# A graph layer on one core: sums in five pieces under a gate, and the products of h moved into the last groups

## The reference

```python
h = jnp.maximum(_layernorm(x, axis=-1), 0.0)                        # 6250 nodes x 64
msg_in = concatenate([h[src], h[dst], edge_attr_32], axis=-1)       # 206250 edges x 160
messages = swish(msg_in @ W1 + b1) @ W2 + b2
att = softmax(swish(msg_in @ Wa1 + ba1) @ Wa2 + ba2, axis=0)        # over all edges
aggregated = segment_sum(messages * att, dst, 6250)
out = x + swish(concatenate([h, aggregated]) @ Wu1 + bu1) @ Wu2 + bu2
```

## Time and profile before

| | |
|---|---|
| runs | 2853.89, 2855.56, 2858.01 us; median 2855.56 |
| profiled execution | 2869.82 us, of which the span is 2868.1 |
| busy | PE 50%, POOL 54%, DVE 36%, ACT 32% of the span |
| granted TensorE clock | 0.629 on average; 0.9 in the first twentieth, then 0.5 to 0.6 |
| moved by DMA | 227.10 MB, 79 GB/s |

### The profile page before, as it was taken

One profiled execution on the slowest core, in us unless ns is written; L12 is line 12 of the kernel. 1 busy time (PEld: TensorE's weight loads), 2 busy tenths in 40 slices (PEclk: granted clock), 3 DMA queues, 4 the chain that ended last, 5 costly groups with the idle time before them and its releaser, 6 DMA issues.

```text
span 2868.1 us, 26391 instructions
## 1 busy us (share of the span) xinstructions
PE 1438.3 (50%) x7070; PEld 1210.3 (42%) x7070; DVE 1031.7 (36%) x2240; ACT 923.1 (32%) x1132; POOL 1540.5 (54%) x1628
## 2 busy tenths in 40 slices
PE   4334454554545455544445554554545444554459
PEld 3334444443444344444344444444444343444444
DVE  6133333343333333333333433333443333333353
ACT  3233333333333333333333333333333333333322
POOL 4355555555555555555555555555555555555520
PEclk9966656566655656565655556556566656566665
DMA  4333333333333333333333333322333333323301
GB/s 123 98 78 83 87 79 78 77 79 78 88 83 79 78 79 77 78 91 80 78 78 80 77 82 89 78 78 77 80 78 87 84 78 78 79 77 78 87 25 23
DMA packets 112463, 227.10 MB, mean 79 GB/s; under 512 B 55880, under 2 KB 76156, under 8 KB 102204
## 3 DMA queue, kind: packets, MB, share of 16 engines
q1 hardware_dynamic: 60376, 121.03, 16.2%
q0 software_dynamic: 51584, 105.75, 15.3%
q10 hardware_dynamic: 484, 0.10, 0.0%
HBM read 218.75 MB, written 8.00 MB: 79 GB/s over the span
## 4 chain that ended last, share of the span: by engine, by line
another core or an unknown queue 57%; DVE 23%; issue 11%; PE 4%; DVEq 3%; DMA 1%; ACT 0%; SPq 0%; ACTq 0%
DVE prod L841 5%; DVE bank L857 5%; DVE v L848 4%; DVE hot L823 3%; DVE lg L843 2%; DVEq L829 1%; PE bank L699 1%; PE bank L713 1%; PE bank L704 1%; PE bank L623 1%; DVE gmax L862 1%; DVE lgb L900 1%; DVE zp L834 1%; PE bank L571 0%
## 5 line engine op out<-in xcount | busy, mean ns | idle before, releaser
L395 POOL DMA_INDIRECT p_rows<-p_tab,src_i x1612 | 1522.3, 944 | 1218.0 <-DMA src_i<-src 716.5
L612 PE MATMUL bank<-q_win,comb 128*128 128x128 f32 x3224 | 862.7, 397 | 939.5 <-issue 925.4
L612 PEld LDWEIGHTS bank<-q_win,comb 128*128 128x128 f32 x3224 | 705.5, 293 | 1066.4 <-issue 1063.8
L501 ACT ACTIVATE s<-bank 128x512 f32<-128x512 f32 x403 | 237.2, 589 | 1736.1 <-DVE bank L857 1735.2
L832 DVE SCALAR_TENSOR_TENSOR acc<-acc,fade,bank 65x96 f32 x81 | 25.1, 310 | 1663.4 <-remote 1613.3
L623 PE MATMUL bank<-hot,v 128*65 128x96 f32 x3224 | 410.6, 306 | 235.0 <-issue 204.4
L623 PEld LDWEIGHTS bank<-hot,v 128*65 128x65 f32 x3224 | 394.2, 185 | 257.7 <-issue 244.4
L857 DVE TENSOR_TENSOR bank<-bank,p_rows 128x512 f32<-128x512 f32 x403 | 278.2, 690 | 12.4 <-PE bank L612 6.5
L471 ACT ACTIVATE comb<-dst_b,row_of 96x1024 f32<-96x1024 int32 (+1 forms) x162 | 217.8, 1344 | 11.4 <-DMA dst_b<-dst_row 11.4
L477 ACT ACTIVATE comb<-comb,ones 96x1024 f32<-96x1024 f32 (+1 forms) x162 | 218.8, 1351 | 2.7
L823 DVE TENSOR_TENSOR hot<-bank,rel 128x960 f32<-128x960 f32 x162 | 185.2, 1144 | 0.0
(11 more groups left out here) (104 smaller groups left out, 449.7 us busy)
## 6 DMA issues: line engine op xcount, KB each, us to landing
dst_b<-dst_row SPq DMA_DIRECT2D x80, 960.0 KB
p_rows<-p_tab,src_i POOLq DMA_INDIRECT x1612
comb<-efT SPq DMA_DIRECT2D x80, 320.0 KB, 3.5
q_win<-q_tab SPq DMA_DIRECT2D x81, 48.0 KB, 2.5
p_tab<-th SPq DMA_DIRECT2D x12, 256.0 KB, 2.3
q_tab<-hot SPq DMA_DIRECT2D x12, 256.0 KB
x_sb<-x SPq DMA_DIRECT2D x3, 512.0 KB, 5.6
out<-s SPq DMA_DIRECT2D x12, 128.0 KB, 2.0
```

Of the source, the lines that this page charges most:

```text
L395: pool.indirect_dma_start(p_rows[:, a, t * H2:(t + 1) * H2], None, p_tab, bass.IndirectOffsetOnAxis(src_i[:, a, t:t + 1], 0)).then_inc(gat ...
L501: nc.scalar.activation(silu_rows(a, q), halves(ps_z[q][:]), ACT.Silu).then_inc(silu_ok, 1)
L612: last = nc.tensor.matmul(ps_z[q][:, (t % TQ) * H2:(t % TQ + 1) * H2], comb[:, a, t * P:(t + 1) * P], q_win[:, a, :], start=True, stop=True)
```

## The change

*Sums in pieces.* The 20 products of `sums` become five calls of four, one per quarter, which add up in the same bank; `hot` and `v` are made per quarter too. Each piece (except in the last group) first waits for a gate: three of the four rows of a quarter of a later group must have landed. For this the fourth row of each quarter gets a semaphore of its own, `gath_end`. Pieces 1 to 4 of g-2 and piece 0 of g-1 are spread over PE's group; `add_part` is now that of g-2 and stands behind logits 3. ACT's `weights` move from behind silu 2 to behind silu 3.

*Products of h.* `own_part` leaves the tail. Its 6272 columns are multiplied in 25 pieces of 256 columns in groups 75 to 79, one per quarter, into the quarter's own bank after its silu; ACT copies each back over `hT`, and the next products in that bank wait for the copy. In the tail DVE adds the products of `acc` to them (`whole_u`), and tanh and silu read `hT`.

*Loops.* Groups 74 to 80 are written out, where 78 to 80 were.

```diff
+        gath_end = [[sem(f"gath_end{a}{q}") for q in range(NQ)] for a in range(2)]
...
+        def own_unit(g, q):
+            u = (g - (LAST - 5)) * NQ + q if isinstance(g, int) and not is_last(g) else -1
+            return [(u, u * 2 * P, min(NP, (u + 1) * 2 * P))] if u >= 0 else []
...
-                    sp.wait_ge(gath[a][NQ - 1], per(a, g, 16 * TQ))
+                    sp.wait_ge(gath[a][NQ - 1], per(a, g, 16 * GQ))
+                    sp.wait_ge(gath_end[a][NQ - 1], per(a, g, 16))
...
-IndirectOffsetOnAxis(src_i[:, a, t:t + 1], 0)).then_inc(gath[a][q], 16)
+IndirectOffsetOnAxis(src_i[:, a, t:t + 1], 0)).then_inc(gath[a][q] if t % TQ < GQ else gath_end[a][q], 16)
...
+            def own_copy(g, q):
+                for u, c0, c1 in own_unit(g, q):
+                    act.wait_ge(uh_done, u + 1)
+                    nc.scalar.activation(hT[0:U, c0:c1], ps_z[q][0:U, 0:c1 - c0], ACT.Copy).then_inc(uh_ok, 1)
...
-            def sums(g):
-                pe.wait_ge(v_ok, g + 1)
-                pe.wait_ge(hot_ok, 2 * g + 2)
-                wait(pe, acc_ok, g)
+            def sums(g, a, c, gate=[]):
+                pe.wait_ge(v_ok, g * NQ + c + 1)
+                pe.wait_ge(hot_ok, g * NQ + c + 1)
+                for gg, aa, qq in gate:
+                    pe.wait_ge(gath[aa][qq], per(aa, gg, 16 * GQ))
+                for t in range(c * TQ, (c + 1) * TQ):
...
             def group(g, a):
+                first = g if isinstance(g, int) else 2
+                def quarter(q):
+                    own_matmul(g, q)
+                    if q < tiles(nxt) // TQ:
+                        for u, _, _ in own_unit(g, q):
+                            pe.wait_ge(uh_ok, u + 1)
+                        zmm(nxt, 1 - a, q)
+                if first > 0:
+                    column_max(g - 1)
+                quarter(0)
+                if first > 1:
+                    sums(g - 2, a, 1, [(g, a, 1)])
+                if first > 0:
+                    spread_max(g - 1)
+                for q in range(1, NQ):
+                    quarter(q)
+                    if q < 4 and first > 1:
+                        sums(g - 2, a, q + 1, [(g, a, q + 1)])
+                    if q == 4 and first > 0:
+                        sums(g - 1, 1 - a, 0, [(nxt, 1 - a, 0)])
...
+            def whole_u(b, a, nt):
+                dve.wait_ge(u_done, b + 1)
+                c = bass.ds(b * NBT * P, nt * P)
+                nc.vector.tensor_tensor(hT[0:U, c], hT[0:U, c], ps_u[a][0:U, 0:nt * P], ALU.add).then_inc(u_ok, 1)
```

More of the change, by code:

```diff
@@ L489, in weights @@
                 nm = neg_max[:, bass.ds(g, 1)]
+                if not (isinstance(g, int) and g == 0):
+                    act.wait_ge(v_ok, g * NQ)
                 act.sem_inc(turn, 1)
@@ L614, in zmm @@
                 last.then_inc(z_done, 1)
[L616 to L624 removed]
+            def sums(g, a, c, gate=[]):
[4 more added lines that the diff above has]
+                for t in range(c * TQ, (c + 1) * TQ):
+                    last = nc.tensor.matmul(ps_part[0:U1, 0:WIN], v[:, t, :], hot[:, t * WIN:(t + 1) * WIN], start=(t == 0), stop=(t == tiles(g) - 1))
+                last.then_inc(sums_done, 1)
             def column_max(g):
@@ L634, in spread_max, with own_matmul @@
                 nc.tensor.matmul(ps_small[:, 0:1], ones[0:1, :], gmax[:], start=True, stop=True).then_inc(maxB_done, 1)
+            def own_matmul(g, q):
+                for u, c0, c1 in own_unit(g, q):
+                    pe.wait_ge(silu_ok, g * NQ + q + 1)
+                    nc.tensor.matmul(ps_z[q][0:U, 0:c1 - c0], wu1h[:], hT[:, c0:c1], start=True, stop=True).then_inc(uh_done, 1)
             def group(g, a):
                 nxt = following(g)[0]
-                late = not (isinstance(g, int) and g == 0)
@@ L639, in group @@
-                quarters = range(tiles(nxt) // TQ) if nxt is not None else []
-                if late:
+                first = g if isinstance(g, int) else 2
[6 more added lines that the diff above has]
+                if first > 0:
                     column_max(g - 1)
-                for q in [q for q in (0,) if q in quarters]:
-                    zmm(nxt, 1 - a, q)
@@ L652, in _, with last_group @@
+            def last_group(g, a):
+                column_max(g - 1)
+                sums(g - 2, a, 1)
+                spread_max(g - 1)
+                for c in range(2, NQ):
+                    sums(g - 2, a, c)
+                for c in range(NQ):
+                    sums(g - 1, 1 - a, c)
             for q in range(NQ):
                 zmm(0, 0, q)
-            groups(pe, group)
+            groups(pe, lambda g, a: last_group(g, a) if is_last(g) else group(g, a))
             column_max(LAST)
@@ L656, in _ @@
             spread_max(LAST)
-            sums(LAST)
+            for c in range(TL // TQ):
+                sums(LAST, 0, c)
             pe.wait_ge(flag_ok, 1)
@@ L1014, in _ @@
             rescale(1, 1, NBT)
+            dve.wait_ge(uh_ok, 5 * NQ)
+            whole_u(0, 0, NBT)
             batches(dve, update)
```

174 lines of the change are left out of this document (102 added, 72 removed).

## The result

The changed kernel takes 2904.37 us (median of 4 runs, 2899.86 to 2909.02) against 2856.08 before: ratio 1.0169, interval [1.0151, 1.0188]. In a second set of runs it was 2903.38 against 2855.04: 1.0165 [1.0148, 1.0181]. The prediction was 2852 and slightly faster. It was wrong in the sign.

The account below looks back on a forecast made before the run. It took the loop as bound by PE's work told late during gathers, no engine full. Loop 0, tail -20, last groups +21, ends -5 from the profiled 2869.8 gave 2865.8; less 14.3 for the median, 2852 us. Range 2190 to 2935.

Parts of the forecast that it names:

- The stop: Each loop group: PE's work told late during POOL's gathers, until 4.8 us after the train; the change leaves it.
- Rival B: Loop: trains close up to POOL's 24.97 us a group, 2221 us in all; chance 0.28 whole, 0.10 in part.
- 33.3 us a group stay: Loop: the period stays 33.3 us, since DVE's added work, gates and semaphore waits cost 0.
- It isn't held.: Loop: DVE's row adds come before the next train's quarters need them, so POOL loses 0 us.
- SP goes on as before.: Loop: products 4 are told done with the rest after the train, so SP continues unchanged, 0 us.
- Rival C: Loop: PE has work left after the train, 2.6 us more a group, 3050 us, or 2951 at half; chance 0.18.
- Tail -20: Tail after the loop: PE bounds it; removing the products with h saves 20 us, bounds -24 and -12.
- Last five groups +21: Groups 75 to 79: products of h with copies add +5 in each of 75 to 77, +3 in 78 and 79.
- Ends -5: First pause shorter by 4 us, and last groups 1 us less from DVE's shorter waits for sums.
- The clock: Tail: PE stays at granted clock 0.50 although busy; by the skill's full-clock rule the saving would be 10 us.

Follow-up runs that it names:

- best_order: Changed kernel with SP's source list load ahead of its wait for products and DVE's first row add directly behind piece 0: 2837.38 us against 2889.47 for the kernel before.
- own_in_last: Kernel before with only the products of h moved into groups 75 to 79, sums kept whole: 2865.34 us against 2855.04, ratio 1.0035.
- before_again: The kernel before itself, no edit, run again for a trace: 2854.58 us against 2855.04.
- fill12: Kernel before with 12 additions of 128x512 on DVE ahead of its add of the sums: 2262.7 us against 2165.85; again, 2857.36 against 2855.04.

## Why the prediction was wrong

*The stop, and that the change leaves it: right.* The stop of PE, its end 4.8 us after the train, DVE's long wait at the new add (17.76 us where I had said about 15) and the trains' pauses are all there. Rival B, that the trains close up, did not happen through the change; on the lower level they are closed for both kernels (25.0 us a group), so the trains close where PE isn't late, with the change or without it.

*Loop "33.3 us a group stay": this step failed.* It was 33.6 against 33.2, 0.44 us a group on average, 31.9 in all. Of it some 0.25 us comes behind the sums' add: POOL starts 5.07 us after it instead of 4.82 or 4.83 (medians of the loop, in both traces of either kernel). Two terms that I had put at nothing make it up:

- *"It isn't held."* I worked out when DVE's row adds of quarters 1 to 4 come, and found none that holds POOL. The one of quarter 0 I left out of that list. Before it stood ahead of the stop; now it stands behind it and ends 4.26 us after the add (median), and POOL issues some 0.8 later.
- *"SP goes on as before."* It goes on 0.16 us later behind the add (0.23 instead of 0.07, medians), since products 4 are now worked off only at the release. The source list lands 4.17 us after the add instead of 3.94, by its semaphore's records, and POOL starts 0.89 after it, as before.

The two come out even: in the group shown the list had landed at 1412.68 and the row add was done at 1412.70, and in 36 of that trace's 72 groups they lie within 0.1 us of each other. The row add is the later one in 44. Each alone gives the whole 5.07 (4.26 + 0.8, 4.17 + 0.89), so by these figures taking away only one would have given nearly nothing back. best_order, which takes away both, starts POOL at 2.92. That the order alone shows a step moved to behind a long wait should have been enough to look for who waits for it.

Another 0.17 us comes before the sums' add (4.79 us after the last issue instead of 4.62). It need not be the change's: two executions of the kernel before differ by as much (4.81 and 4.62), and that is where the profiled execution that I predicted from had its 14 us above the median of the runs.

*Rival C, PE left with work:* nothing like its 2.6 us a group; at most the 0.17 is what there is of it. My reason against it was misread: of the records at the end of the stop the trace before has six, from 1439.03 to 1441.2, and no 12 that went in 0.9 us.

*Tail -20: right.* -18.8, a batch of 3.80 us where I had 3.75.

*Last five groups +21: mis-sized.* The mechanism was the one named. By own_in_last the three groups with a train behind them cost 18.2 (I had 15; a round trip and the products around it come to 6 us, not 5), and the two behind cost 11.6 where I had 6: 30 in all. That DVE's work hides less of the copies than I took would explain the last figure, but it isn't shown.

*Ends -5: mis-sized.* The beginning gave -5.3 where I had -4: POOL's first long pause is 11.42 us of idle time instead of 15.68, and the next is short.

```profile
205.28 0.95 POOL L402 DMA_INDIRECT p_rows<-p_tab,src_i  x1 [11.42 <-DMA src_i<-src]
...
235.31 0.95 POOL L402 DMA_INDIRECT p_rows<-p_tab,src_i  x1 [5.32 <-DMA src_i<-src]
```

The end, where I had -1, costs some +9: 20.8 us more to the last add against 11.6 with the products of h alone. More pieces than I counted, which lag by two groups now, are left behind the last train; that this makes the difference is argued from the order and not shown. With +5.1 in the three periods (23.3 against 18.2) the change costs 14 us there beyond the products of h alone; by the other trace (18.0 and 19.9) it is 8.

Sum: -5.3 + 31.9 + 23.3 + 20.8 - 18.8. What was meant to be even (+21 and -20) became +30 and -19, and the sums in pieces, with whatever they and the products of h do to each other, added 42 (51.9 less 9.6) that I had put at -5.

The range: my bounds of 2825 to 2885 for the forecast were not the sum of the parts' bounds. Added plainly these give 2820 to 2895, and 2933 with the 0.5 us a group that I had allowed for DVE's instructions. The measured 2904 lies within the last of these alone. And C at half its price (2951) lies above the 2935 at which I ended the whole range.

The clock: the batch lost 1.71 us (5.51 to 3.80), nearly the removed product's whole 1.76, and the granted clock in the tail after is 0.50 again (2860 to 2890). I had set the Trainium skill's rule ("TensorE: Matmul & The Clock Gate", the part on the clock gate) aside for the tail because the rows had 0.50. By that rule the batch would have lost some 0.9, an estimate from the 1.76; the trace doesn't agree with it.

What stays open: why PE and SP are late under gathers at one level and not at the other. One chip had both, so it isn't the chip alone. Open too is what the sums in pieces cost by themselves at the upper level, and whether either of the two moved steps, taken alone, gives anything back there.

## What to carry to other kernels

When an order is changed around a long wait, list everything that has moved from ahead of it to behind it, and for each who waits for it; here two such steps, each put at nothing, cost 0.25 us in each of 72 groups, and since they ended together neither would have shown by itself. Work spread over the last rounds of a loop in small pieces with a copy back is cheap only if each piece's round trip is hidden: here 25 pieces gave 19 us and cost 30 where PE was late, and gave 15 net where it wasn't (by difference of two versions). And a wait that the profile can give to nobody may be a property of the run and not of the kernel; such a kernel is worth a second measurement before anything is built on its period.

## What the runs showed of the hardware

- The same kernel took 2855, 2889 or 2166 to 2169 us in different sets of runs; within a set the runs of a kernel lie within 0.4% of each other. On the upper level many matmuls start in steps of 0.70 us while POOL issues gathers and for some 3 us after the last, and SP's register instructions take up to 1.4 us; the durations on DVE and POOL are not touched. What PE has done is also told late: the sums' last record ends 19.0 us (median, before_again) before DVE's add. On the lower level PE did 79 records in a 25 us window with gathers all the time.
- A change can have opposite signs on the two levels: 1.0165 and 0.9915.
- A gather's issue on POOL took 1.15 us instead of 0.94 while DVE added two operands from SBUF. The gathers then stand 1.45 us apart, twice the 0.725 from one addition to the next, and most end about 0.1 us after an addition's end (fill12, fill12_again). The Trainium skill (SBUF — State Buffer, SBUF: two separate sides) says that such an operation contends with GpSimd's reads; the trace agrees, and the 0.2 us look like a wait for the running addition's end.
- By the sentence of the Trainium skill quoted ahead (SBUF — State Buffer, SBUF: two separate sides), that a DMA and a compute operation don't slow each other, PE wouldn't be late under gathers. The lower level agrees: 79 records in 25 us with gathers all the time. On the upper level PE is late under the same gathers; whether they are the cause isn't shown.
